# A transformer layer on one core: row maxima of four heads taken in the first stage, the others as an even stream on four PSUM banks

## What is computed

```python
x = L0_attn_hidden_states                      # [4, 2048, 256]
xn = _layernorm(x, axis=-1)
# attention: 16 heads of 16, a bias by relative position
qkv = hidden_states @ W_qkv
scores = jnp.einsum('bhqd,bhkd->bhqk', q, k)
scores = scores + compute_bias(rel_emb, S, S)
attn = jax.nn.softmax(scores.astype(jnp.float32), axis=-1)
out = jnp.einsum('bhqk,bhkd->bhqd', attn, v)   # then @ W_out
# feed-forward, scaled by the sum of the normalised top-2 router weights
expert_out = jnp.matmul(jax.nn.gelu(jnp.matmul(xt, w1) + b1), w2) + b2
out = expert_out * jnp.sum(combine, axis=-1, keepdims=True)
x = x + attention(xn) + ffn(xn)
```

## Time and profile before

| | |
|---|---|
| median of 3 runs | 3267.45 us (3267.31 to 3268.53) |
| the profiled execution | 3269.68 us, its span 3267.8 us |
| TensorE busy | 3200.7 us, 98% |
| VectorE busy | 2813.3 us, 86% |
| ScalarE busy | 2439.0 us, 75% |
| GpSimd busy | 1297.9 us, 40% |
| mean granted clock of TensorE | 0.994 of full |

### The profile page before, as it was taken

How to read it: one execution, slowest core, us unless ns; L and a number is a source line. 1 busy time by engine, 2 the same in 40 slices (tenths; PEclk the granted TensorE clock), 3 DMA queues, 4 the chain that set the end, 5 groups by cost and what they waited for, 6 DMA issues and landing times.

```text
span 3267.8 us, 72368 instructions
## 1 busy us (share of the span) xinstructions
PE 3200.7 (98%) x28170; PEld 1717.4 (53%) x28170; DVE 2813.3 (86%) x3760; ACT 2439.0 (75%) x4667; POOL 1297.9 (40%) x1918
## 2 busy tenths in 40 slices
PE   7999999799999999999999999999999999999997
PEld 6888889344444444444444444444444444444446
DVE  5577765699999999999999999999999999999922
ACT  4443344588888888888888888888888888888883
POOL 1212112344444444444444444444444444444445
PEclk9999999899999999999999999999999999999999
DMA  8532232432222222221122222212222221222105
GB/s 194 123 91 78 78 108 87 78 66 37 37 37 37 37 37 37 37 37 37 37 37 37 37 37 37 37 37 37 37 37 37 37 37 37 37 37 37 23 10 186
DMA packets 136725, 175.46 MB, mean 54 GB/s; under 512 B 53008, under 2 KB 100816, under 8 KB 130048
## 3 DMA queue, kind: packets, MB, share of 16 engines
q1 hardware_dynamic: 136384, 170.83, 25.6%
HBM read 110.31 MB, written 56.69 MB: 51 GB/s over the span
## 4 chain that ended last, share of the span: by engine, by line
PE 77%; DVE 3%; DMA 2%; issue 1%; SPq 0%; POOL 0%; ACT 0%; DVEq 0%; ACTq 0%
PE ps L1108 27%; PE ps L1125 24%; PE ps L1097 18%; PE ps L1130 8%; DVE max_half L1042 2%; DMA out_rows<-base_in 1%; PE ps L1165 0%; DMA k_st<-base_in 0%; DMA base_in<-base_rows 0%; SPq L194 0%; POOL prob L1007 0%; DVE neg_turn L1055 0%; SPq L860 0%; POOL turned L1015 0%; ACT turned L967 0%
## 5 line engine op out<-in xcount | busy, mean ns | idle before, releaser
L1042 DVE TENSOR_REDUCE max_half<-ps 128x1 f32<-128x512 f32 (+1 forms) x2666 | 2398.1, 945 | 121.5 <-PE ps L1097 118.1
L960 ACT ACTIVATE prob<-ps 128x512 f32<-128x512 f32 x4096 | 2156.3, 600 | 440.4 <-PE ps L1108 428.4
L1007 POOL TENSOR_TENSOR prob<-prob,near 128x224 f32<-128x224 f32 (+2 forms) x1664 | 978.3, 603 | 1450.9 <-ACT prob L960 1444.6
L1108 PE MATMUL ps<-q_st,k_st 49*128 49x512 f32 x4096 | 1407.3, 442 | 21.4 <-DMA k_st<-base_in 21.1
L1097 PE MATMUL ps<-k_st,q_st 48*128 48x512 f32 x3968 | 1403.2, 450 | 8.5 <-DVE max_half L1042 7.1
L1108 PEld LDWEIGHTS ps<-q_st,k_st 49*128 49x128 f32 x4096 | 658.8, 184 | 747.3 <-ACT prob L960 681.1
L1125 PE MATMUL ps<-prob,vr 128*32 128x384 f32 x4864 | 756.3, 498 | 0.0
L1097 PEld LDWEIGHTS ps<-k_st,q_st 48*128 48x128 f32 x3968 | 636.9, 184 | 180.7 <-DVE max_half L1042 103.3
L1125 PE MATMUL ps<-prob,vx 128*32 128x384 f32 x3328 | 593.5, 499 | 1.1 <-issue 1.1
L1125 PEld LDWEIGHTS ps<-prob,vr 128*32 128x32 f32 x4864 | 133.4, 108 | 325.5 <-issue 221.4
L662 PE MATMUL ps<-xnt,w_parts 128*128 128x512 f32 x1152 | 275.4, 398 | 8.7 <-DVE parts L512 5.1
(11 more groups left out here) (70 smaller groups left out, 1161.6 us busy)
## 6 DMA issues: line engine op xcount, KB each, us to landing
qk_parts<-parts SPq DMA_DIRECT2D x64, 512.0 KB, 4.7
q_st<-qk_parts SPq DMA_DIRECT2D x192, 128.0 KB, 3.9
k_st<-qk_parts SPq DMA_DIRECT2D x192, 128.0 KB, 5.4
near<-bias_near SPq DMA_DIRECT2D x64, 352.0 KB, 6.2
x_sb<-in_L_attn_hidden_states SPq DMA_DIRECT2D x18, 512.0 KB, 6.1
base_rows<-x_sb SPq DMA_DIRECT2D x16, 512.0 KB, 2.9
recip_rows<-recip_all SPq DMA_DIRECT2D x256, 32.0 KB, 1.8
base_in<-base_rows SPq DMA_DIRECT2D x16, 512.0 KB, 5.7
```

The costliest lines, as they stand in the source:

```text
L960: nc.scalar.activation(prob[:, t % PROBS, CH * j:CH * (j + 1)], ps[:, bank_of(at)], ACT.Exp).then_inc(drained, 1)
L1007: nc.gpsimd.tensor_tensor(at, at, near[n % GROUP][:, side, c0:c0 + q1 - q0], ALU.mult).then_inc(near_done, 1)
L1042: nc.vector.tensor_reduce(max_half[:, m % 2].rearrange("p i c -> p (i c)")[:, k:k + len(banks)], tiles, AX.X, ALU.max) \
L1108: nc.tensor.matmul(ps[:, bank_of(at)], k_st[u][:, P * kb:P * (kb + 1)], q_st[u][:, CH * c:CH * (c + 1)], start=True, stop=True).then_inc(s ...
```

## The change

- Early maxima: heads 0 to 3 instead of 0 and 1, in two passes of two heads, one in chunks 4 to 7 and one in 8 to 11, 16 pieces a chunk. The pieces stand in nine places of a chunk, seven with two and two with one, on the bank pairs 0-1, 4-5 and 6-7 (EARLY_F1, EARLY_F2); each waits for the reduction of the last piece in its banks. The wait for the last reductions of a chunk moves to the next chunk's first F1 product.
- The low parts of the hidden layer are subtracted by GpSimd instead of VectorE, the power of the norm between the second and the third.
- The other 60 heads' maxima run as one stream over the score tiles of 63 heads less the last eight visits, with a fixed plan: in a visit of three, a single tile in bank 3 of the four and then a pair, in banks 1, 2 and 0, 1 by turns; the tile in the shared bank 1 is made last. A pair doesn't span two heads.
- Scores and maxima have stacks of their own, two each, loaded one head ahead. Combining comes one visit after a head's last reduction, turning one later (TURN_LATER). The scores keep three banks to the end.

The diff, cut to its core:

```diff
-GROUP = 4
-GROUPS = NH // GROUP
-LEAD = 2
+STACKS = 2
+NEARS = 4
+NEGS = 6
...
+EARLY_PASSES = B - 2
+EARLY_HEADS = 2 * EARLY_PASSES
+EARLY_PASS = KB * CPB
+EARLY = EARLY_PASSES * EARLY_PASS
+EARLY_IN_CHUNK = EARLY_PASS // CPB
+EARLY_F1 = {1: [(0, 0), (1, 6)], 3: [(2, 0), (3, 6)], 5: [(4, 0), (5, 6)], 7: [(6, 0)]}
+EARLY_F2 = {(0, 3): [(7, 4)], (0, 7): [(8, 0), (9, 4)], (1, 7): [(10, 0), (11, 4)], (2, 7): [(12, 0), (13, 4)], (3, 7): [(14, 0), (15, 4)]}
+EARLY_BANK = dict(pair for slot in [*EARLY_F1.values(), *EARLY_F2.values()] for pair in slot)
+EARLY_BEFORE = {piece: max((p for p in range(piece) if EARLY_BANK[p] == bank), default=None) for piece, bank in EARLY_BANK.items()}
...
+SPARE = 8
+SINGLE = CPB - 1
+SHARED = 1
...
+    groups, in_visit, ends = [], [], {}
+    wanted, slots = CPB * KB * (NH - EARLY_HEADS), CPB * KB * (NH - 1) - sum(len(visit) for visit in VISITS[NV - SPARE:])
+    passed = done = pairs = 0
+    for t in range(NV * NH):
+        passed = min(passed + len(VISITS[t % NV]), slots)
+        take = wanted * passed // slots - done
+        tiles = []
+        while take > 0:
+            m, k = EARLY_HEADS + done // (CPB * KB), done % (CPB * KB)
+            size = 1 if take != 2 or k == CPB * KB - 1 else 2
+            at = len(groups)
+            first = SHARED - pairs % 2
+            banks = range(first, first + 2) if size == 2 else range(SINGLE, SINGLE + 1)
+            pairs += size == 2
+            for i in sorted(range(size), key=lambda i: banks[i] == SHARED):
+                tiles.append((m, k + i, banks[i], freed[banks[i]], at))
+            for bank in banks:
+                freed[bank] = at
+            groups.append((m, k, banks))
+            if k + size == CPB * KB:
+                ends[m] = t, at
+            done += size
+            take -= size
+        in_visit.append(tiles)
+    assert done == wanted
+    return groups, in_visit, ends
+MAX_GROUPS, MAX_IN_VISIT, MAX_ENDS = max_groups()
+TURN_LATER = 2
...
+                def hid_lows(n):
+                    for f in range(KF):
+                        if f == 2:
+                            norm(n + 1)
+                        wait(pool, hid_high, KF * n + f + 1)
+                        if f == 0:
+                            wait(pool, f2_ready, TPC * n)
+                        nc.gpsimd.tensor_tensor(hid[:, 1, f], hid_raw[:, f % RAWS], hid[:, 0, f].bitcast(F32), ALU.subtract).then_inc(hid_low, 1)
...
+                for n in range(B * CPB):
+                    hid_lows(n)
+                    exps(n)
...
+                        if not first:
+                            if m == 0:
+                                wait(dve, f2_copied, TPC * n)
+                            add_base(n - 1, (c - 1) % CPB, m)
+                    if first:
+                        w_low_part(W_2)
                     norm_stats(nb, ncc)
+                    norm_var(n + 1)
                     for f in range(KF):
-                        if f == 1:
-                            norm_var(n + 1)
-                        if f == KF // 2:
+                        if f == 4:
                             scale(nb, ncc)
-                        wait(dve, hid_high, KF * n + f + 1)
-                        if f == 0:
-                            wait(dve, f2_ready, TPC * n)
-                        nc.vector.tensor_tensor(hid[:, 1, f], hid_raw[:, f % RAWS], hid[:, 0, f].bitcast(F32), ALU.subtract).then_inc(hid_low, 1)
-                        if f < TPC and not first:
-                            add_base(n - 1, (c - 1) % CPB, f)
-                        if first and f == 0:
-                            w_low_part(W_2)
+                        if early and f in EARLY_F1:
+                            for piece, _ in EARLY_F1[f]:
+                                early_max(b, c, piece)
...
+                        if t == TPC - (2 if last else 1):
+                            scales(n)
                         if early:
-                            early_max(b, c, 2 * t + 1)
+                            for piece, _ in EARLY_F2[t, 7]:
+                                early_max(b, c, piece)
...
+                    if c == 0 and piece == 0:
+                        pe.wait_ge(early_in[b - 1], 2 * 16 * STACK_LOADS)
+                    if EARLY_BEFORE[piece] is not None:
+                        wait(pe, max_done, early_first(b, c) + EARLY_BEFORE[piece] + 1)
+                    elif bank == 6:
+                        wait(pe, lo_done, 2 * KE * (CPB * b + c + 1))
+                    elif bank == 4:
+                        wait(pe, gelu_done, KF * (CPB * b + c + 1))
                     for h in range(2):
-                        last = nc.tensor.matmul(ps[:, h], query_block(q_early[HALF * h:HALF * h + ROWS], i),
-                                                k_early[HALF * h:HALF * h + ROWS, CH * j:CH * (j + 1)], start=True, stop=True)
+                        last = nc.tensor.matmul(ps[:, bank + h], query_block(q_early[b - 1][HALF * h:HALF * h + ROWS], i),
+                                                k_early[b - 1][HALF * h:HALF * h + ROWS, CH * j:CH * (j + 1)], start=True, stop=True)
                     last.then_inc(max_ready, 1)
...
+                        if f == 0 and (early or c == 0 and b > 0):
+                            wait(pe, max_done, early_first(b, c))
...
-            q_two = [sb(f"q_st{i}", [P, S], F32R, c=c2) for i in range(GROUP // 2)]
-            k_two = [sb(f"k_st{i}", [P, S], F32R, c=c2) for i in range(GROUP // 2)]
-            q_st, k_st = ([two[u % 2][HALF * (u // 2):HALF * (u // 2) + ROWS + 1] for u in range(GROUP)] for two in (q_two, k_two))
-            near = [sb(f"near{u}", [P, 2, NT], c=c2) for u in range(GROUP)]
+            q_two = [sb(f"q_st{i}", [P, S], F32R, c=c2) for i in range(STACKS)]
+            k_two = [sb(f"k_st{i}", [P, S], F32R, c=c2) for i in range(STACKS)]
+            q_score, k_score = ([stack[0:ROWS + 1] for stack in two] for two in (q_two, k_two))
+            q_max, k_max = ([stack[HALF:HALF + ROWS] for stack in two] for two in (q_two, k_two))
...
                 for n in range(NH):
-                    if n + GROUP - 1 < NH:
-                        load(n + GROUP - 1)
-                        load_near(n + GROUP - 1)
+                    turned_by = turned_in(n + 1) < NV * n if n + 1 < NH else None
                     if n + 1 < NH:
+                        load(n + 1)
+                    if turned_by is True:
                         shift(n + 1)
+                    load_maxima(NV * (n - 1) + NORM_AT, NV * n)
+                    if n + NEARS - 1 < NH:
+                        load_near(n + NEARS - 1)
                     if n > 0:
                         totals(n - 1)
                         spread(n - 1)
+                    load_maxima(NV * n, NV * n + TOTAL_AT)
+                    if turned_by is False:
+                        shift(n + 1)
+                    if n > 0:
                         keep(n - 1)
+                    load_maxima(NV * n + TOTAL_AT, NV * n + NORM_AT)
...
+                    for v in range(NV):
+                        t = NV * n + v
+                        for at in sorted({tile[-1] for tile in MAX_IN_VISIT[t]}):
+                            maxima(at)
+                        for m in range(EARLY_HEADS, NH):
+                            if t == MAX_ENDS[m][0] + TURN_LATER - 1:
+                                combine(m)
+                            if t == MAX_ENDS[m][0] + TURN_LATER:
+                                turn(m)
...
+                def maxima(m, k, bank, before, at, last):
+                    if MAX_GROUPS[at][1] == 0:
+                        pe.wait_ge(max_in[m % STACKS], 16 * STACK_LOADS * ((m - EARLY_HEADS) // STACKS + 1))
                     wait(pe, max_done, EARLY + before + 1 if before >= 0 else 0)
-                    u = m % GROUP
-                    mm = nc.tensor.matmul(ps[:, MAX_BANK + bank], query_block(q_st[u][0:ROWS], k // CPB),
-                                          k_st[u][0:ROWS, CH * (k % CPB):CH * (k % CPB + 1)], start=True, stop=True)
+                    mm = nc.tensor.matmul(ps[:, MAX_BANK + bank], query_block(q_max[m % STACKS], k // CPB),
+                                          k_max[m % STACKS][:, CH * (k % CPB):CH * (k % CPB + 1)], start=True, stop=True)
                     if last:
                         mm.then_inc(max_ready, 1)
...
+                        tiles = MAX_IN_VISIT[t]
+                        for j, (kb, c) in enumerate(visit):
                             scores(n, kb, c)
-                            if m < NH:
-                                maxima(m, TILE[kb, c])
-                        t = NV * n + v - LAG
-                        if t >= 0:
-                            sums(t // NV, t % NV)
+                            if j < len(tiles):
+                                at = tiles[j][-1]
```

(1 more changed line is left out.)

220 lines of the change are left out of this document (93 added, 127 removed).

## The result

The changed kernel takes 3296.49 us (median of 4 runs, 3293.04 to 3301.88), beside 3267.38 for the kernel before: a ratio of 1.0091, 95% interval 1.0073 to 1.0108. It is slower by 0.9%, where 3240 was forecast, and outside the range of 3204 to 3264.

A forecast was written before the change was run, and what follows sets the result against it. TensorE and VectorE, both nearly full, were taken to wait for each other at bank hand-overs. Gains of 49.4, 1.2 and 1.3 us less losses of 23 and 1 gave 27.9 us, hence 3240 us, range 3204 to 3264.

The forecast's parts named there:

- The banks: Attention stage: with the new order bank 1 comes free 0.1 us before needed, so the hand-over bubble of 0.23 us goes.
- rival (a): Attention visits: bank 1's hand-over sets a slower pace; at 0.05 us a visit the time is 3304 us; 10 in 100.
- The stream of maxima: Attention stage: fewer maxima tiles a score bring VectorE to 37.7 us a head, under TensorE's 39.1 without waits.
- TensorE itself at 1.81: Attention stage: once the bubble is gone, TensorE's own pace of 1.81 us a visit is the next limit.
- Three singles: Visits near head ends with only single tiles, all in bank 3: 1.8 us each in 16, 0.6 in 4, 31 lost.
- Last heads: Heads 61 to 63: head 61 becomes 39.4 us, head 62 becomes 38.0, and the last gets 1 us longer.
- start of stage: Start of the attention stage: two rows of ones instead of four sent through SyncE's queue, 1.2 us gained.
- SyncE's queue: Attention heads: 21 issues take 13.0 us before the totals, against 16.3 until VectorE's reciprocal; hidden.
- Early pieces: First stage: 16 pieces in nine places cost 2.9 us more a chunk, 23 lost, plus 1; chunk 12's stall gives 1.3.
- Subtractions on GpSimd: First stage, all 16 chunks: eight subtractions at 1.284 us hidden by 1.3 us, cost 0; upper bound 20 us.
- (b): Attention stage: part of the bubble stays, 0.3 us more a head, 3258 us; 12 in 100.
- (c): First stage: early pieces cost 0.61 us each or VectorE misses two places a chunk, 16 to 20 more, 3258; 10 in 100.

The follow-up runs named there:

- b_banks: The kernel before with only the order of the maxima banks changed (single tile first in bank 3, then the pair): 3202.14 us, ratio 0.9793.
- e11_uneven: b_banks with VectorE's reductions reading only 32 of 512 columns in every third visit of a head: 3198.34 us in one run.
- e7_half_read: b_banks with each reduction of max tiles in the attention stage reading only 256 of 512 columns: 3082.36 us in one run.
- e12_twos_f2: b_banks with its eight early pieces a chunk in four places of two, all in the second product group: 3186.37 us, ratio 0.9751.
- e9_narrow: The changed kernel with three-single visits spread over three banks and GpSimd subtracting only 32 of 512 columns after the first chunk: 3217.76 us.
- b_gpsimd: The kernel before with only the subtractions of the hidden layer's low parts moved to GpSimd: 3270.75 us, ratio 1.0002.
- e4_vector_low: The changed kernel with three-single visits spread over three banks and the low-part subtractions back on VectorE: 3310.28 us, ratio 1.0129.

## Why the prediction was wrong

*What bounds the kernel.* Right as far as it went: two engines waited for each other at the hand-over of banks, by 1.65 us a head.

*The banks.* Right. The bubble went, bank 1 was in time, and rival (a) didn't come true: b_banks shows 8.1 us of waiting in some 60 heads.

*The stream of maxima.* Here the reasoning failed. "It is no longer as slow as TensorE" compared averages, 37.7 against 39.1. A visit with a pair and a single still asks 1.817 us of VectorE, and what a lighter visit saves is idle time (e11_uneven). "TensorE itself at 1.81" was not TensorE's own pace either: that of the rest is 1.72 (e7_half_read). The text named this as what would fell it. The size was hardly touched: 39.67 instead of 39.4, 60 x 0.27 = 16 us. But it follows that the whole of the early work for heads 2 and 3, priced at 24 us of loss, bought 60 x 0.04 = 2.4 us, and the last three heads took that back.

*Three singles.* The step that failed most is the price of these visits, which held the stall and no clock. The stall was priced at 1.8 us; the three heads whose clock stayed took 41.69 in the mean, 2.02 more than the others: 32.3 us in 16 visits instead of 28.8. The four visits of two lost 2.7 instead of 2.4. What was missed is what follows: the other 13 heads took 578.5 us in all and so lost another 36.5 (578.5 less 13 x 41.69) to the half clock. It is the largest missed term. The trace of before held waits of TensorE that were short and single; I didn't ask what two longer ones in a row, with little between, do to the clock.

*The sum of 60 heads.* Forecast 49.8 gained, measured 6.0 lost: 16 of that from the pace, 4 from the stalls, 36 from the clock.

*Last heads, start of stage, SyncE's queue.* Heads 61 to 63 lost 1.4 where 0.4 was summed. From chunk 15 to head 0 nothing was gained: TensorE's wait before the stage's first matmul, which the profile puts down to the ones row, is 21.35 us against 21.08, though the two loads fewer did halve their time in SyncE's queue (1.22 us instead of 2.48). So that time is not what the wait depends on, a step that failed by 1.2 us; what it does depend on stays open. SyncE's queue was hidden as forecast: VectorE's reciprocal waits for the totals only twice, as in the kernel before. The end of the kernel is 2.8 us shorter and its first two chunks are 2.5 us shorter, which I hadn't forecast and haven't traced. With these the misses add up: 55.8 in the 60 heads, 7.5 in the early chunks (below), 1.2 and 1.0 here, less 2.8 and 2.5, are the 60.2 us between the forecast span of 3239.9 and the 3300.1 of the profile.

*Early pieces.* The eight early chunks, the stall at chunk 12 among them, cost 30.2 us instead of 22.7. The matmuls were overpriced: a place of two costs (34.97 - 31.68) / 4 = 0.82 us (e12_twos_f2), the second piece thus 0.21 and not 0.33, and with the hold-up taken away (e9_narrow) the sum would have been about 18. The missed term is VectorE's lateness. My layout of its queue had the normalising at 1.4 us, and margins of 0.1.

*Subtractions on GpSimd.* "Hidden, so I take 0" holds for GpSimd, whose operations took 1292 ns. What it does to VectorE was put at nothing: beside it the four normalising operations take 4.00 us instead of 1.38, 2.6 us a chunk more, and GpSimd's own are longer by next to nothing (1319 ns in b_gpsimd against 1284). I weighed only GpSimd's standstill. The rule of the Trainium skill that I set against the move (SBUF — State Buffer, Who interferes with whom) covers both: whichever of the two engines issues first gets the shared pair, and the other is the one that blocks. The trace agrees that the two hold each other up, with VectorE as the one that is held here. It cost 12 to 15 us instead of 1 or 2, and since the 16 pieces need the move (e4_vector_low), it belongs to their price.

*The rivals.* (b) had the right size for the 60 heads' pace (18 us against 16), and (c) part of the right size for the early chunks; they could have been taken together. None of them had the clock. The chance of a slower kernel rested on (a), which didn't come; the kernel got slower by other mechanisms.

So the change holds one part worth 65 us, the bank order. The rest buys 2.4 us in the 60 heads, and costs 2.9 in the last three, some 30 in the first stage and 72 in the visits of singles.

## What to carry to other kernels

Where two nearly full engines hand over a few banks, compare them visit by visit and not by averages: relief in some visits is worth next to nothing when the ring holds only one visit, and the order of the ring can be worth more than any work moved away. Price a new wait of TensorE twice, as a stall and as the half-clock stretch that can follow it, and price an engine given new work also by what it does to its neighbour's operations.
